# Second pair's last norm taken by feature: one transpose of the sums instead of two, means and scales laid along rows through DRAM

## What is computed

```python
x = x + rwkv_block(layernorm(x))        # norms, r/k/v/o products, channel mix with a 512 -> 2048 -> 512 MLP
z = (x - mean(x)) / sqrt(var(x) + eps)  # the last norm, over the 512 features of each token
gate_up = z @ w_gate_up.T               # 512 -> 2 x 2048
gate, up = split(gate_up)
out = x + (silu(gate) * up) @ w_down.T  # 2048 -> 512
```

## Time and profile before

| | before |
|---|---|
| median of 3 runs (lowest to highest) | 1058.92 us (1058.69 to 1059.34) |
| the profiled execution's own time | 1058.57 us |
| its span | 1056.8 us |
| PE busy | 1048.6 us, 99% of the span |
| DVE, ACT, POOL busy | 683.0, 520.2, 589.3 us |

### The profile page before, as it was taken

The page is one execution under the profiler, slowest core; times in us unless marked ns, Lnnn a source line. Parts: engine busy times, 40 slices in busy tenths (PEclk is TensorE's granted clock), DMA queues, the critical chain, the costliest instruction groups (busy, mean ns, idle before and its releaser), DMA issues.

```text
span 1056.8 us, 13615 instructions
## 1 busy us (share of the span) xinstructions
PE 1048.6 (99%) x4744; PEld 868.6 (82%) x4744; DVE 683.0 (65%) x1213; ACT 520.2 (49%) x881; POOL 589.3 (56%) x492
## 2 busy tenths in 40 slices
PE   8999999999999999999999999999999999999999
PEld 6888888788888888888888888888888888888887
DVE  7887757786545564565459666776558566666665
ACT  7867576766444354323355433333445344444442
POOL 7776283735765545444447755564563265655552
PEclk9999999999999999999999999999999999999999
DMA  8002052277653344742323666555436445454432
GB/s 322 1 1 41 1 136 59 86 214 277 236 182 127 130 160 134 231 152 92 121 79 110 239 219 219 193 189 196 171 136 210 131 152 196 149 160 160 153 107 80
DMA packets 45380, 157.21 MB, mean 149 GB/s; under 512 B 4096, under 2 KB 4480, under 8 KB 40704
## 3 DMA queue, kind: packets, MB, share of 16 engines
q1 hardware_dynamic: 29856, 108.02, 29.2%
q0 software_dynamic: 15168, 48.24, 15.2%
q10 hardware_dynamic: 288, 0.09, 0.0%
HBM read 97.60 MB, written 58.72 MB: 148 GB/s over the span
## 4 chain that ended last, share of the span: by engine, by line
PE 94%; POOL 3%; DVE 2%; DMA 0%; ACT 0%; issue 0%; SPq 0%; ACTq 0%; DVEq 0%
PE bank L589 14%; PE bank L591 14%; PE bank L590 14%; PE bank L578 14%; PE bank L579 14%; PE bank L580 14%; PE bank L775 2%; PE bank L774 2%; PE bank L773 2%; POOL operand L1913 2%; POOL weights L1901 1%; PE bank L653 1%; PE bank L754 1%; POOL weights L1913 0%; PE bank L819 0%; PE bank L821 0%
## 5 line engine op out<-in xcount | busy, mean ns | idle before, releaser
L589 PE MATMUL bank<-combo,left 128*128 128x512 f32 x672 | 262.5, 391 | 0.4 <-DVE bank L1647 0.4
L591 PE MATMUL bank<-combo,left 128*128 128x512 f32 x672 | 261.7, 389 | 0.0
L590 PE MATMUL bank<-combo,left 128*128 128x512 f32 x672 | 261.6, 389 | 0.0
L1592 DVE TENSOR_TENSOR resid<-bank,resid 128x512 f32<-128x512 f32 x176 | 120.4, 688 | 143.3 <-PE bank L580 142.5
L1965 POOL TENSOR_TENSOR inner<-made,inner 128x512 fp32r<-128x512 f32 x96 | 125.6, 1330 | 130.0 <-ACT inner L1086 130.0
L1935 POOL TENSOR_TENSOR left<-quart,left 128x512 fp32r<-128x512 f32 x96 | 114.8, 1219 | 86.7 <-ACT left L1051 48.0
L578 PE MATMUL bank<-right,inner 128*128 128x512 f32 x384 | 149.6, 390 | 0.0
L579 PE MATMUL bank<-right,inner 128*128 128x512 f32 x384 | 149.5, 389 | 0.0
L580 PE MATMUL bank<-right,inner 128*128 128x512 f32 x384 | 149.5, 389 | 0.0
L589 PEld LDWEIGHTS bank<-combo,left 128*128 128x128 f32 x672 | 126.2, 188 | 27.4 <-DVE bank L1647 1.1
L591 PEld LDWEIGHTS bank<-combo,left 128*128 128x128 f32 x672 | 126.2, 188 | 26.2
(11 more groups left out here) (187 smaller groups left out, 1929.5 us busy)
## 6 DMA issues: line engine op xcount, KB each, us to landing
kept_left<-left SPq DMA_DIRECT2D x24, 1792.0 KB, 8.1
left<-kept_left POOLq DMA_DIRECT2D x24, 1024.0 KB, 7.1
left<-kept_left POOLq DMA_DIRECT2D x24, 768.0 KB, 5.1
quart<-wide SPq DMA_DIRECT2D x24, 512.0 KB, 4.1
tall_staged<-tall SPq DMA_DIRECT2D x48, 256.0 KB, 5.2
raw<-kept SPq DMA_DIRECT2D x32, 256.0 KB, 6.1
landed<-wts SPq DMA_DIRECT2D x20, 256.0 KB, 5.9
resid<-x POOLq DMA_DIRECT2D x4, 1024.0 KB, 9.7
```

The costliest lines, as they stand in the source:

```text
L589: pe.matmul(acc[:], hi, combo[:, c, k, 0, :], start=fresh and k == 0, stop=False, skip_group_check=True)
L590: pe.matmul(acc[:], hi, combo[:, c, k, 1, :], start=False, stop=False, skip_group_check=True)
L591: mm = pe.matmul(acc[:], lo, combo[:, c, k, 0, :], start=False, stop=k == 1, skip_group_check=True)
L1592: dve.tensor_tensor(tile, A[s][:], tile, ALU.add).then_inc(added, 1)
```

## The change

For blocks 2 and 3 the sums x are transposed once, right after their statistics (units 24 and 28), from `resid` into the banks A and back into `resid`, by feature. The norm is then done on them by feature. Mean and scale of a token are then no longer numbers per partition but run along the row, the same for all partitions: DVE puts the means and POOL the scales in `row_stats` (128 x 2 x 4), SP stores them to a small DRAM tensor `rows` (256 pieces of 16 bytes) and reads it back to all 128 partitions into `extra` (2 x 512 columns per partition, 512 KB in all). A piece of 4 values belongs to one partition, so along the tokens of one tile the values stand 4 apart, and DVE reads them with a step of 16 bytes. `norm3_rows` is two instructions of DVE per tile (subtract, then multiply), where `norm3` was one. The transposes of z for blocks 2 and 3, the later `turn` and ACT's copies of one of them are gone. The first pair is as before.

```diff
-NORM3_UNIT = tuple(piece_unit(j, NORM_PIECES - 1) + 1 for j in range(BLOCKS))
+NORM3_UNIT = tuple(piece_unit(j, NORM_PIECES - 1 if j < PAIRS else SUBS) + 1 for j in range(BLOCKS))
-TURN_UNIT = {2: 28, 3: FIRST[3] + 1}
-TURN_AFTER = {j: tiles_in(u, 1)[0] for j, u in TURN_UNIT.items()}
+        row_stats = sb("row_stats", [P, 2, SUBS])
+        rows = nc.dram_tensor("rows", (PAIRS, 2, BT), F32, kind="Internal").ap()
...
+            def keep_rows(j):
+                sp.wait_ge(ln_rstd, 2 * BLOCKS + j)
+                sp.wait_ge(ln_stats, SUBS * (2 * BLOCKS + j + 1) + j - PAIRS + 1)
+                sp.dma_start(rows[j - PAIRS].rearrange("n (p s) -> p n s", s=SUBS), row_stats[:]).then_inc(rows_moved, 16)
+
+            def load_rows(j):
+
+                sp.wait_ge(rows_moved, 32 * (j - PAIRS) + 16)
+                sp.wait_ge(z3_ready, SUBS * j)
+                sp.dma_start(extra[:], rows[j - PAIRS:j - PAIRS + 1].broadcast_to((P, 2, BT))).then_inc(rows_moved, 16)
...
+                for j in range(PAIRS, BLOCKS):
+                    if u == NORM3_UNIT[j]:
+                        keep_rows(j)
+                        load_rows(j)
...
             def norm3(j):
-                pe.wait_ge(z3_ready, SUBS * (j + 1))
+                if j < PAIRS:
+                    pe.wait_ge(z3_ready, SUBS * (j + 1))
+                else:
+                    pe.wait_ge(x2_moments, SUBS * (j + 1))
+                source = fin[j % 2] if j < PAIRS else resid[:, j]
                 for n in range(NORM3_AFTER[j], NORM3_AFTER[j] + SUBS):
                     s = n % SUBS
                     pe.wait_ge(added, n - SUBS + 1)
                     for k in range(KT):
-                        mm = pe.transpose(A[s][:, k * P:(k + 1) * P], fin[j % 2][:, s, k * P:(k + 1) * P], ident[:])
+                        mm = pe.transpose(A[s][:, k * P:(k + 1) * P], source[:, s, k * P:(k + 1) * P], ident[:])
                     mm.then_inc(t3_psum, 1)
-
-            def turn(j):
...
             def norm3(j):
                 act.wait_ge(t3_psum, SUBS * (j + 1))
+                place_of = raw[j] if j < PAIRS else resid[:, j]
...
             def x2_stats(j):
-                if j:
+                if j == BLOCKS - 1:
+                    dve.wait_ge(rows_moved, 16)
+                elif j:
                     dve.wait_ge(z3_ready, SUBS * j)
...
+                if j >= PAIRS:
+                    dve.tensor_copy(row_stats[:, 0, :], stats2[:, :, 0]).then_inc(ln_stats, 1)
                 dve.tensor_scalar(var_eps[:, 0], stats2[:, :, 1], EPS, None, ALU.add).then_inc(ln_var, 1)
...
+            def norm3_rows(j, k):
+
+                dve.wait_ge(t3_kept, SUBS * (j + 1))
+                dve.wait_ge(rows_moved, 32 * (j - PAIRS + 1))
+                tile, before = (t.rearrange("q (s p) -> q s p", s=SUBS) for t in (raw[j % 2][:, k, :], resid[:, j, k, :]))
+                mean, scale = (extra[:, n, :].rearrange("q (p s) -> q s p", s=SUBS) for n in range(2))
+                dve.tensor_tensor(tile, before, mean, ALU.subtract).then_inc(z3_part, 1)
+                dve.wait_ge(z3_part, KT * (j - PAIRS) + k + 1)
+                dve.tensor_tensor(tile, tile, scale, ALU.mult).then_inc(z3_ready, 1)
...
                             if piece > SUBS:
-                                norm3(j, 2 * (piece - SUBS - 1))
-                                norm3(j, 2 * (piece - SUBS - 1) + 1)
+                                tile = norm3 if j < PAIRS else norm3_rows
+                                tile(j, 2 * (piece - SUBS - 1))
+                                tile(j, 2 * (piece - SUBS - 1) + 1)
...
+                scale = row_stats[:, 1, :] if n >= 2 * BLOCKS + PAIRS else rstd2[:]
+                pool.tensor_tensor(scale, var_eps[:, 0], minus_half[:, 0], ALU.pow).then_inc(ln_rstd, 1)
```

More of the change, by code:

```diff
@@ L427, in build @@
         out_stored = sem("out_stored")
-        turn_psum, turned = sem("turn_psum"), sem("turned")
+        z3_part, rows_moved = sem("z3_part"), sem("rows_moved")
         side_sums, side_hi, side_lo = sem("side_sums"), sem("side_hi"), sem("side_lo")
@@ L733, in out_tile @@
                 after = [j for j in range(BLOCKS) if NORM3_AFTER[j] <= n < NORM3_AFTER[j] + SUBS]
-                turn = [j for j in TURN_AFTER if TURN_AFTER[j] <= n < TURN_AFTER[j] + SUBS]
                 if after:
                     pe.wait_ge(t3_kept, SUBS * after[0] + n - NORM3_AFTER[after[0]] + 1)
-                elif turn:
-                    pe.wait_ge(turned, SUBS * (turn[0] - 2) + n - TURN_AFTER[turn[0]] + 1)
                 elif n >= SUBS:
@@ L753, in norm3 @@
                     for k in range(KT):
-                        mm = pe.transpose(A[s][:, k * P:(k + 1) * P], fin[j % 2][:, s, k * P:(k + 1) * P], ident[:])
+                        mm = pe.transpose(A[s][:, k * P:(k + 1) * P], source[:, s, k * P:(k + 1) * P], ident[:])
                     mm.then_inc(t3_psum, 1)
-            def turn(j):
-                pe.wait_ge(z3_ready, SUBS * (j + 1))
-                for n in range(TURN_AFTER[j], TURN_AFTER[j] + SUBS):
-                    s = n % SUBS
-                    pe.wait_ge(added, n - SUBS + 1)
-                    for k in range(KT):
-                        mm = pe.transpose(A[s][:, k * P:(k + 1) * P], resid[:, j, s, k * P:(k + 1) * P], ident[:])
-                    mm.then_inc(turn_psum, 1)
             def side_product(acc, q, a, c, fresh):
@@ L882, in unit @@
                         norm3(j)
-                for j in TURN_UNIT:
-                    if u == TURN_UNIT[j]:
-                        turn(j)
                 if q > 0:
@@ L1077, in combo_hi_of @@
                     act.wait_ge(raw_back[1], 16)
+                elif stage == 2:
+                    act.wait_ge(t3_kept, 2 * SUBS)
                 else:
-                    act.wait_ge(t3_kept, 2 * SUBS * (stage - 1))
+                    act.wait_ge(z3_ready, SUBS * BLOCKS)
                 for k in range(2):
@@ L1150, in plain_right_hi @@
                     act.activation(plain_right[:, i, 0, :], plain_staged[:, i, :], ACT.Copy).then_inc(down_hi, 1)
-            def turn(j):
-                act.wait_ge(turn_psum, SUBS * (j - 1))
-                for n in range(TURN_AFTER[j], TURN_AFTER[j] + SUBS):
-                    s = n % SUBS
-                    act.activation(resid[:, j, :, s * P:(s + 1) * P], A[s][:].rearrange("p (k t) -> p k t", k=KT),
-                                   ACT.Copy).then_inc(turned, 1)
             def gated_hi(u):
@@ L1546, in right_sums @@
                     dve.wait_ge(raw_back[1], 16)
+                elif stage == 2:
+                    dve.wait_ge(t3_kept, 2 * SUBS)
                 else:
-                    dve.wait_ge(t3_kept, 2 * SUBS * (stage - 1))
+                    dve.wait_ge(z3_ready, SUBS * BLOCKS)
                 raw0, raw1 = right_raw(stage, 0), right_raw(stage, 1)
@@ L1611, in x2_stats @@
                     dve.bn_aggr(stats2[:, s, :], moments[:, s, :]).then_inc(ln_stats, 1)
-                dve.wait_ge(ln_stats, SUBS * (2 * BLOCKS + j + 1))
+                dve.wait_ge(ln_stats, SUBS * (2 * BLOCKS + j + 1) + max(j - PAIRS, 0))
+                if j >= PAIRS:
+                    dve.tensor_copy(row_stats[:, 0, :], stats2[:, :, 0]).then_inc(ln_stats, 1)
                 dve.tensor_scalar(var_eps[:, 0], stats2[:, :, 1], EPS, None, ALU.add).then_inc(ln_var, 1)
@@ L1698, in add_x @@
                 dve.wait_ge(o2, q + 1)
-                dve.wait_ge(turned, 2 * SUBS)
+                dve.wait_ge(t3_kept, SUBS * BLOCKS)
                 side_add(OX, 0, q % 2, ox_added)
@@ L1811, in unit @@
                     combo_lo_of(after, T1)
+                last_norm(u, 1)
                 if u in SUMS_UNIT and not is_key(u):
                     right_sums(SUMS_UNIT.index(u))
-                last_norm(u, 1)
             first_norm1()
```

3 lines of the change are left out of this document (1 added, 2 removed).

## The result

The changed kernel takes **1061.37 us** (median of 14 runs, 1059.76 to 1062.37) against 1059.03 us for the kernel before, run beside it (14 runs, 1058.38 to 1059.90). The ratio is 1.0021 with a 95% interval of 1.0012 to 1.0029: slower by 2.3 us, a small difference, but one whose interval leaves out 1. The forecast of 1055.7 us is missed by 5.7 us; the range holds the time only because it reached into rival 1.

A forecast was written before the change was run, and what follows sets the result against it. PE was taken as the bound, busy 1048.6 of 1056.8 us. 1058.57 (profiled execution) - 3.54 (transposes) + 0.3 (stall) = 1055.33, so 1055.7 us for a median; range 1054.7 to 1064.0.

The forecast's parts named there:

- rival 1: DVE's norm: the 16-byte step halves the pace, 0.53 us more an instruction; 1057.8 us without POOL turns, 1065.5 with; chance 0.43.
- What DVE gets: DVE's norm, units 24, 25, 28, 29: four instructions take 2.64 us, 1.73 more, if the step is free; +0.3 us overall.
- Two groups of transposes: On PE, two groups of 16 transposes fewer, at 1.77 us each: -3.54 us.
- ACT's copies: Eight ACT copies of 512 columns go; PE is not waiting for ACT there, so they count as nothing.
- The norm at unit step: DVE's four norm instructions at the pace of `make_x2`'s rows: 2.64 us, 1.73 more than now.
- the turn with POOL: After the norm in units 24 and 25, L1600 waits behind a POOL subtraction and starts at about 703.8.
- the limit for `seed`: In unit 25 `seed` must start by 705.79 or PE waits; it was expected at 705.6.
- The 0.15 us of stall a unit: `sum_v` expected at 709.8 against a limit of 709.87; 0.15 us in each of two units, +0.3 us.
- The rows through DRAM: Store 3.5 us, read 4.1 us; rows there at 694.6 to 696.3, wanted at 700.95, so no wait.
- rival 2: The rows come late through DRAM, so PE stands 2 to 3 us in one or two units: 1058 to 1061; chance 0.05.
- rival 3: Unit 34's first products wait for copies and subtractions, so removing unit 33's group gains nothing: 1057.4 us; chance 0.05.

The follow-up runs named there:

- experiment 1: The change, but DVE reads the rows one after the other (step of 4 bytes), giving tokens other tokens' values: 1055.66 us, ratio 0.9967.
- experiment 2: The change, but DVE reads the rows at a step of 8 bytes, with other tokens' values: 1055.23 us, ratio 0.9964.
- experiment 3: The change with each norm instruction cut in two, 340 columns at 12 bytes and 172 in a row, other tokens' values: 1059.69 us, single run.
- experiment 4: The change, but ACT writes the transposed sums 4 columns apart, DVE reads in a row, the host reorders output columns: 1055.64 us, ratio 0.9967.
- experiment 5: The change with its 16-byte step, but block 2's norm one tile a unit in units 24 to 27: 1055.43 us, ratio 0.9966.
- experiment 9: The change, but rows stored in 512 pieces of 8 bytes, so DVE reads values 2 apart, right result kept: 1055.52 us, ratio 0.9966.
- experiment 10: The change with rows stored in 8-byte pieces and block 2's norm one tile a unit in units 24 to 27: 1055.52 us, ratio 0.9966.
- experiment 11: The change with ACT writing 4 columns apart, DVE reading in a row, and block 2's norm one tile a unit: 1055.75 us, ratio 0.9967.
- experiment 6: The kernel before, plus three idle DVE instructions with a 16-byte operand at the ends of units 24 and 25: 1067.03 us, ratio 1.0077.
- experiment 8: The change, but at the end of units 24 and 25 DVE does block 3's three instructions before block 2's norm: 1061.34 us, ratio 1.0021.
- experiment 7: The kernel before, plus three idle DVE instructions with a 16-byte operand at the end of unit 24 only: 1063.16 us, ratio 1.0040.

## Why the prediction was wrong

**The step that failed** is under "What DVE gets": "Four take 2 x (0.71 + 0.61) = 2.64 us if the step of 16 bytes costs nothing". It does not cost nothing. An instruction takes 1.07 us in place of 0.68, the four 4.23 us. The condition was written down, and the chances for and against it were nearly even, but the wrong side was taken, with the argument that the nearest rows are `make_x2`'s. Those rows have the operation and the size, but not the step; on the point in dispute they were no neighbour at all. The rule of the Trainium skill ("Advanced Engine Details and Errata", section on SBUF cachelines) that each line of 16 bytes wants two reads was cited in the prediction and spoke for the rival; experiments 1 to 3 agree with it. Rows that say nothing on a point leave it open; they are no reason to take the cheap side.

**Point by point.**

- Two groups of transposes, -3.54 us: right. Those of units 30 and 33 are each seen in the timeline as 1.77 us, and every version without such waits lands near it (experiments 1, 2, 4, 5, 9 to 11): the medians are 3.2 to 3.9 us under the kernel before, and in the traces `seed` of unit 34, less what the start scatters, is 3.4 to 3.6 us earlier.
- ACT's copies at nothing: right, PE waits for none of them.
- The norm at unit step, the turn with POOL and the limit for `seed`: right in mechanism and size, as experiment 1 shows (2.66 us for 2.64, one turn, 1.46 us late where the prediction had 1.59, and no wait). The 0.15 us of stall a unit that I took for `sum_v` didn't come.
- Rival 1 is what happened, with its sign: PE's products of S1 in units 25 and 26 wait for DVE L1658. Its size was wrong. Its price was half the pace, 0.53 us more an instruction, taken from POOL's pace; measured are 0.39 (1.07 against 0.68 us). It gave the norm three turns in units 24 and 25; there were two. The fourth norm instruction started at 705.12, 0.10 us before POOL, where the dearer one would have come behind it. In units 28 and 29 it had a turn and 0.75 us of delay in each; there the fourth also starts just ahead of POOL, the output tile comes 0.7 us late and the idle time in front of `seed` swallows it. So two waits of 2.2 us stood in for 4.3 + 4.3 + 0.75 + 0.75, and the time is 1061.4 in place of 1065.5 us. That it came within the stated range is no merit of the forecast's mechanism.
- A term that neither case had: the clock. The two waits and the transposes alone give -3.54 + 4.44 = +0.90 us. Three of the change's 14 runs have a mean clock of 1.000 and take 1059.76, 1059.76 and 1060.16 us, 0.7 to 1.1 above the kernel before. The other eleven are at 0.998, with a median of 1061.58 us, 2.5 above. Without the slower products the change would hardly be told from the kernel before.
- The rows through DRAM: the store took 4.5 to 5.3 us where I chose 3.5, and the read 3.9 for 4.1. The rows came at 698.6, which is 697.6 without the late start and not 696.3, and 3.3 us before DVE wanted them. Rivals 2 and 3 did not happen: DVE is never idle in front of L1631, and the group of unit 33 gives its 1.77 us to the next unit's `seed`.

## What to carry to other kernels

Before you cost an instruction by its neighbours in the trace, check that they have its access pattern too, not only its shape and operation; an fp32 operand read 16 bytes apart cost 1.6 times the instruction here and one 8 bytes apart nothing, so a layout that leaves two neighbours together is enough. Ask then how much room the place has: the same slow instructions of block 2 cost 5.7 us where two tiles stood together and nothing where they stood one to a unit. And a wait of some 2 us of a PE that was busy all the time can cost twice, once for itself and once, in most executions here, for the clock behind it.

## What the runs showed of the hardware

- DVE, 512 columns of fp32 with two SBUF operands: 0.68 us with steps of 4 or 8 bytes, 1.06 to 1.09 with one operand at 16; 12 bytes stands between (1.03, 1.32 and 1.76 ns a column for 8, 12 and 16 bytes, the last two in the ratio of the 16-byte lines touched). ACT pays 1.125 in place of 0.602 us for writing 16 bytes apart.
- A DVE instruction with two SBUF operands and POOL's subtractions go by turns, one instruction each, and each pays about 1.0 to 1.1 us (DVE, 1.80 for 0.68) or 0.65 us (POOL, 3.86 for a pair of 2.55) a turn. DVE's norm by token, which reads one tile and two columns of numbers per partition, was held too (experiment 6, 1.41 us for 0.55); `accumulate`, which reads one operand from PSUM, was not (0.67 us at 710.16, with POOL at work). The Trainium skill ("SBUF — State Buffer", section on the two sides of SBUF) has the shared port pair as a lock that one of the two holds for the whole instruction; the traces agree, with two turns in either order of DVE's work (experiment 8).
- PE's clock fell from 2.4 to 1.2 GHz for some 3 us, beginning 1.1 us after the end of a wait of 2.06 us. By its mean clock it fell in 11 of 14 runs of the change, in 7 of 10 of experiment 8, in 4 of 4 of experiment 6 and in 2 of 4 with a single wait of 2.9 us (experiment 7). A second wait of 2.05 us, 19 us later, was not followed by it, nor were two waits of 1.2 us each in the one run of experiment 3. What decides between one execution and the next was not found.
- A store of 4 KB to DRAM took 2.2 to 5.6 us in 256 pieces of 16 bytes over the kernels here (16 stores), and 4.2 to 5.9 us in 512 pieces of 8 bytes (4 stores).
